# Three of a pair's sixteen maxima, issued in front of the values two pairs ahead

## What is computed

```python
q, k, v = x_norm @ Wq, context @ Wk, context @ Wv      # 8 heads of 64
attn = softmax(q @ k.T * 64 ** -0.5)                    # per batch and head, 256 x 1601
x = x + (attn @ v) @ Wo + bo
# then layernorm, a router (top 2 of 8), 8 experts and a shared one of 128 -> 256 -> 128
x = x + shared + mixed
```

## Time and profile before

| | |
|---|---|
| median of 3 runs | 413.12 us (412.89 to 413.26) |
| the profiled execution, device time | 414.8 us |
| its span, first to last instruction | 412.9 us |
| TensorE busy | 404.6 us (98%) |
| VectorE, ScalarE, GpSimd busy | 267.0, 248.2, 270.3 us (65%, 60%, 65%) |
| TensorE's share of the chain that ended last | 94% |

### The profile page before, as it was taken

The page is one execution under the profiler, slowest core; times in us unless marked ns, Lnnn a source line. Parts: engine busy times, 40 slices in busy tenths (PEclk is TensorE's granted clock), DMA queues, the critical chain, the costliest instruction groups (busy, mean ns, idle before and its releaser), DMA issues.

```text
span 412.9 us, 9465 instructions
## 1 busy us (share of the span) xinstructions
PE 404.6 (98%) x3590; PEld 334.7 (81%) x3590; DVE 267.0 (65%) x565; ACT 248.2 (60%) x399; POOL 270.3 (65%) x182
## 2 busy tenths in 40 slices
PE   7999999999999999999999999999999999999996
PEld 6787888797878887979779878888697777878886
DVE  5986878586626766857347667873585747557644
ACT  5677556382865554638737455467381736789883
POOL 6429788897913988567319793847075890498881
PEclk9999999999999999999999999999999999999999
DMA  6600002000000020000000120000000003202400
GB/s 209 175 1 2 2 2 62 2 2 2 0 2 2 3 61 1 2 2 2 1 2 3 59 61 2 2 2 0 2 3 2 0 3 103 102 2 71 148 14 27
DMA packets 17140, 11.75 MB, mean 28 GB/s; under 512 B 10188, under 2 KB 14136, under 8 KB 17096
## 3 DMA queue, kind: packets, MB, share of 16 engines
q1 hardware_dynamic: 17096, 11.15, 10.1%
HBM read 10.55 MB, written 0.56 MB: 27 GB/s over the span
## 4 chain that ended last, share of the span: by engine, by line
PE 94%; ACT 2%; DVE 1%; issue 1%; DMA 1%; POOL 0%; ACTq 0%; DVEq 0%
PE ps L1186 23%; PE ps L1170 16%; PE ps L1019 11%; PE ps L1020 10%; PE ps L1021 10%; PE ps L1111 8%; PE ps L1161 6%; PE ps L1049 4%; PE ps L1057 2%; PE ps L1118 2%; ACT probs L797 1%; ACT xn L720 1%; DMA x_sb<-in_x_dram 1%; DVE xn L877 0%; PE ps L1134 0%
## 5 line engine op out<-in xcount | busy, mean ns | idle before, releaser
L797 ACT ACTIVATE probs<-ps 128x1024 f32<-128x1024 f32 (+1 forms) x112 | 105.7, 963 | 114.4 <-PE ps L1170 111.3
L914 DVE TENSOR_REDUCE maxes<-ps 128x1 f32<-128x402 f32 x256 | 132.5, 570 | 44.8 <-PE ps L1111 40.1
L483 POOL TENSOR_TENSOR work<-work,probs 128x1024 f32<-128x1024 f32 x60 | 142.8, 2380 | 4.7
L1186 PE MATMUL ps<-probs,v_sb 128*64 128x256 f32 (+1 forms) x832 | 94.3, 384 | 0.0
L481 POOL TENSOR_TENSOR work<-probs 128x1024 f32<-128x1024 f32 x15 | 36.0, 2398 | 87.4 <-issue 75.4
L1186 PEld LDWEIGHTS ps<-probs,v_sb 128*64 128x64 f32 (+1 forms) x832 | 58.8, 138 | 31.8 <-issue 3.9
L1170 PE MATMUL ps<-kq_hi,kq_lo 64*128 64x256 f32 (+1 forms) x416 | 70.1, 280 | 0.0
L1170 PE MATMUL ps<-kq_lo,kq_hi 64*128 64x256 f32 (+1 forms) x416 | 70.0, 279 | 0.0
L1170 PE MATMUL ps<-kq_hi 64*128 64x256 f32 (+1 forms) x416 | 69.8, 278 | 0.0
L911 DVE TENSOR_TENSOR kq_lo<-ps,kq_hi 128x402 fp32r<-128x402 f32 (+2 forms) x80 | 41.7, 543 | 35.2 <-ACT kq_hi L745 33.8
L1111 PE MATMUL ps<-kq_hi 64*128 64x402 f32 x256 | 60.2, 365 | 0.1
(11 more groups left out here) (151 smaller groups left out, 655.3 us busy)
## 6 DMA issues: line engine op xcount, KB each, us to landing
v_sb<-weight_rows SPq DMA_DIRECT2D x12, 256.0 KB, 3.8
raw<-in_ctx_T_dram SPq DMA_DIRECT2D x3, 600.4 KB, 4.6
work<-in_L_ffn_rw_dram SPq DMA_DIRECT2D x1, 1024.0 KB, 6.9
shift_rows<-neg_row SPq DMA_DIRECT2D x64, 0.5 KB, 2.0
raw<-weight_rows SPq DMA_DIRECT2D x4, 256.0 KB, 3.5
raw<-in_ctx_T_dram SPq DMA_DIRECT2D x3, 150.8 KB, 2.9
x_sb<-in_x_dram SPq DMA_DIRECT2D x1, 384.0 KB, 6.6
wo_sb<-in_L_xattn_Wo_dram SPq DMA_DIRECT2D x1, 256.0 KB, 8.0
```

What stands on the lines that cost most here:

```text
L483: ops.tensor_tensor(acc, acc, pr, ALU.add).then_inc(summed, 1)
L797: nc.scalar.activation(dst, src, ACT.Exp, scale=SCALE).then_inc(probs_ready, 1)
L914: v.tensor_reduce(maxes[:, p % 2, i * T + t, blk:blk + 1], src[:, 0:BW], AX.X, ALU.max).then_inc(ring_taken, 1)
L1186: ins = mm(o_bank[DH * i:DH * (i + 1), :], v_sb[0:rows, c, h * DH:(h + 1) * DH], probs[0:rows, n % SLOTS, i, j * S:(j + 1) * S], start=(c ...
```

## The change

For the first pair nothing moves. From then on, three of the 16 maxima of pair n+2, which stood behind pair n's values and in front of pair n+1's scores, stand in front of pair n's values (and in front of the step `add`). Behind each of the first six units two maxima follow, as before, and one behind the seventh. That is so for 14 pairs' values, 0 to 13. In pairs 4, 8 and 12 the order of the `v` projections among the others shifts as well: before, the list ran `k v v q v v spread v v k v v k v v k v v v`; now it runs `v v v k v v q v v spread v v k v v k v v k`, so that a `k` comes last. No instruction is added or taken away on any engine.

```diff
     for n, (b, p) in enumerate(order):
         ahead = maxima[n + 1] if n + 1 < n_order else []
-        out += ahead[:3]
+        out += ahead[:3] if n == 0 else []
         for u in range(n_units):
             out.append(("scores", (b, p, u)))
             out += ahead[2 * u + 3:2 * u + 5]
@@
         if vs:
-            for i, x in enumerate(projections or vs[:1]):
-                out += ([x] if projections else []) + vs[2 * i:2 * i + 2]
-            out += vs[2 * len(projections or vs[:1]):]
+            for i, x in enumerate(projections):
+                out += vs[2 * i + 1:2 * i + 3] if i else vs[:3]
+                out.append(x)
@@
         out += [("w1", k) for k, at in enumerate((0, 2, 3)) if n == at]
+        if n + 2 < n_order:
+            out += maxima[n + 2][:3]
         out.append(("add", (b, p)))
         out += [("values", (b, p, u, j)) for u, unit in enumerate(key_units(chunks)) for j in range(len(unit))]
```

## The result

The changed kernel takes 427.31 us (median of 4 runs) where the kernel before took 413.19 in the same comparison: ratio 1.032, 95% interval 1.026 to 1.039. It is slower, as forecast, but by 14 us instead of 6.7, and outside the range of 417.4 to 423.0. The profiled execution took 427.94 us with a span of 426.2. Medians here are over all executions, while a ratio and its interval leave out those more than 1.5% above the fastest of the same kernel, so the two can differ a little.

A forecast was written before the change was run, and what follows sets the result against it. TensorE, last in the chain for 94% of the span, bounds the kernel. 14.6 us lost in front of the values minus 7.9 saved behind is +6.7, so 413.12 + 6.7 = 419.8 us; range 417.4 to 423.0.

The forecast's parts named there:

- the chain and the terms: Chain that ended last is TensorE for 94% of the span; other engines count only where TensorE waits for them.
- Savings behind the values: From values' end through the scores: 5.0 us before unit 0, 3.9 in unit 1, less 1.0 given back, 7.9 saved.
- unit 0 as worked out: From values' end to unit 0's last product: 0.87 us instead of 1.23, 0.36 a pair, 5.0 us over 14 pairs.
- unit 1 as worked out: Fourth and fifth maximum find banks free, so unit 1 takes 1.13 us, not 1.41: 0.28 a pair, 3.9 us.
- late units 2 and 4: Units 2, 4 and 6 wait for the exponential, 1.20 us instead of 1.13; one more 0.07 a pair, 1.0 us.
- the ring: Before values in pairs 1, 5, 6, 9, 10, 13, third maximum waits for its bank: 3.0, 0.9 or 2.2 us each.
- the fronts: Extra time before the values over 14 pairs: 4.6 with free banks, 4.4, 2.6 and 3.0 with waits, 14.6 us.
- pair 11, counted as free: Before pair 11's values, nothing slow stands in front because its router result is small: 0.57 us more, no wait.
- the form change: Around the values three changes of matmul form instead of two, 0.10 us each; with free banks 0.57 more in front.
- the clock behind the new waits: At the new waits in pairs 1, 6, 10, the summed forecast included no further clock fall; chance 0.66.
- Rival (a): Clock falls at new waits, pair 1 first, 1.7 us each: one fall gives 421.5, three 424.9; chance 0.18.

The follow-up runs named there:

- only where the bank is free: Changed kernel, three maxima moved only in pairs 0, 2, 3, 4, 7, 8, 11, 12: 414.66 us, ratio 1.0006 to the kernel before.
- two in front of the values: Changed kernel with two maxima instead of three before the values, the third placed behind the seventh unit: 421.55 us, ratio 1.016 to the kernel before.
- The waits alone: Kernel before, no maximum moved, TensorE made to wait before the values of pairs 1, 6 and 10: 426.13 us, ratio 1.024.
- filled: Changed kernel with 19 idle matmuls issued into the long waits of pairs 1, 6 and 10: 421.92 us, ratio 1.017 to the kernel before.
- the changed kernel again: Changed kernel, unchanged, run for more executions and a second profile: 425.8 us, ratio 1.020 to the kernel before.

## Why the prediction was right in sign and wrong in size

**Right: the chain and the terms.** Savings behind the values were forecast at 7.9 us and measured at 8.5: unit 0 as worked out (0.87), unit 1 as worked out (1.13), and late units 2 and 4, but hardly 6 (0.02), so that less was given back than the 0.07 a pair.

**Right: the ring.** The six pairs, their releasers and their lengths came as worked out: 0.97 for 0.9 in pairs 5, 9 and 13, 2.3 for 2.2 in pairs 6 and 10, 3.1 for 3.0 in pair 1. That the loss is gone when the six pairs are left as they were (only where the bank is free), and that the waits of pairs 5, 6, 9, 10 and 13 are gone without the third maximum (two in front of the values), shows the cause. Summed, the fronts cost 15.5 us for 14.6; pair 11, counted as free, took 0.72.

**Right in sum, not shown in its reason: the form change.** 0.57 in front of the values with free banks was measured at 0.56 to 0.61, and where nothing waits the move earns nothing (only where the bank is free, 1.0006). The Trainium skill (TensorEngine Tiling, "Key Properties") says that a change of tiling mode drains the array. The steps from a projection to a maximum and from a lone maximum to the values, 0.27 to 0.28 us against 0.18 between like matmuls, agree with it. But 0.10 is not the price of every change: from two maxima to the values it takes 0.37, and from the first two maxima to a third of the same form 0.28. No run here separates a drain from another reason for these steps.

So 6.7 was 7.1 in the profile's stages and 6.6 to 7.3 between executions at full clock: 420.14, in the one execution of that kind, for a forecast of 419.8.

**A reading that was off.** The prediction puts the 1.7 us between the profiled 414.8 and the median of 413.12 down to what lies around the span. Going by the other executions of the kernel before, they are rather the one fall of the clock in pair 14: at a mean clock of 1.000 it mostly took 412.9 to 414.3 us, at 0.996 mostly 414.6 to 415.6. The clocks of the three runs behind 413.12 are not known. The forecast itself starts from the median and is not touched. But against that median the changed kernel's fall at pair 14 counts as well: 6.7 and four falls of up to 1.7 make up to 13.5, close to the 14 between the medians.

**Wrong: the clock behind the new waits, a term put at nothing.** The sum has no fall of the clock in it; measured are three, which made the values of pairs 1, 6 and 10 longer by 4.8 us. Rival (a) had the price right, 1.7 us a fall, and the places. The step that failed is its weighing: "Against it: at the other shorter waits of this trace the clock stays." I gave it 0.18 and let the range hold one fall. But the longest wait of TensorE in that trace behind the first 10 us was 0.72 us, and behind it the clock did fall; no wait of 1.4 us or more spoke for its staying up. The forecast should have been the case with falls, at 421.5 to 425, and the range up to 425. The waits alone, without a moved maximum, brought three falls; filled, the same waits brought none. In pair 1 the clock fell in all four profiles of kernels that have its wait unfilled. In pairs 6 and 10 it fell in one and in two of the changed kernel's two.

**Outside of the forecast.** 1.5 us of the profile's 13.3 came from a late rise of the clock at the start. The second profile does not have it, and nothing in the change reaches there. Why the clock fell behind the same 1.45 us wait in one execution and not in the next I can't say from these runs; what TensorE did before both is the same to 0.05 us. The 0.72 us wait of pair 14 is as undecided: it is in all ten profiles, and the clock fell behind it in six (not in those of the free banks, the filled waits, the waits alone, and the changed kernel again).

## What to carry to other kernels

A step moved past a long stretch of work gives up the cover that this stretch gave to the buffer it needs: look up who used that buffer last, and when it is released, at the new place and not at the old one. A new wait of TensorE, where it is the busiest engine, may have to be priced twice, once for itself and once for the clock behind it: here 1.7 us behind nine of ten waits of 1.4 to 2.6 us, and behind six of ten of 0.72. And tiny moves add up at the joints: here a step from one form of matmul to another took 0.1 to 0.2 us more than one between like matmuls, and a lone maximum took as long as two side by side (0.18 us saved behind the seventh unit without it).

## What the runs showed that was not expected

- The clock fell behind the router's twelve short matmuls (pair 11) with hardly a wait, in one profile of the changed kernel and in that of the filled one. In both TensorE is shown as busy throughout; ahead of the fall at pair 14 stood eight row sums of one column and the wait of 0.72. No run here tells why. Each fall made the values 1.7 us longer where all of it lay in them.
- Two maxima alone between two other forms are followed by the next form after 0.37 us; a third one behind them after 0.27. Three thus cost 0.57 in front of the values and two 0.38.
- At the start the profile's clock line shows 1.00 while matmuls of 402 columns follow each other after 0.34 us; only their pace, against 0.19, shows that the array was slow.
